# Attention heads paired across two key groups, and the spread of the inverse row sums on VectorE

## What is computed

```python
def _L0_attn_ref(X, Wq, Wk, Wv, Wpost):      # 16 heads in 4 groups
    Q = (X @ Wq).reshape(n, s, 4, 4, 64)     # (group, head of the group, width)
    K = (X @ Wk).reshape(n, s, 4, 64)        # one key and one value per group
    V = (X @ Wv).reshape(n, s, 4, 64)
    raw = einsum('bsgwe,btge->bstgw', Q, K / 8)
    attn = softmax(raw, axis=2)
    A = einsum('bstgw,btge->bsgwe', attn, V).reshape(n, s, 1024)
    return X + A @ Wpost

x = x + attention(xn) * silu(mixture_of_64_experts(xn))       # layer 0
x = x + state_space_model(xn) * silu(forest_of_8_trees(xn))   # layer 1
```

## Time and profile before

| | |
|---|---|
| median of three runs | 2696.54 us (2693.64 to 2705.16) |
| profiled execution, its own time | 2710.37 us |
| span of the profile | 2708.3 us |
| PE, matmuls (busy) | 2271.3 us, 84% of the span |
| DVE (VectorE) | 1850.7 us, 68% |
| ACT (ScalarE) | 1767.2 us, 65% |
| POOL (GpSimd) | 1738.4 us, 64% |
| PE clock granted, mean | 0.94 |

### The profile page before, as it was taken

How to read it: one execution, slowest core, us unless ns; L and a number is a source line. 1 busy time by engine, 2 the same in 40 slices (tenths; PEclk the granted TensorE clock), 3 DMA queues, 4 the chain that set the end, 5 groups by cost and what they waited for, 6 DMA issues and landing times.

```text
span 2708.3 us, 38199 instructions
## 1 busy us (share of the span) xinstructions
PE 2271.3 (84%) x13192; PEld 1417.2 (52%) x13192; DVE 1850.7 (68%) x2832; ACT 1767.2 (65%) x3278; POOL 1738.4 (64%) x1416
## 2 busy tenths in 40 slices
PE   5777879999688889799989898989888988987781
PEld 4444557775444456455644465546544644554351
DVE  5778544543246786687578766876777667788888
ACT  3556534446277876788677867785887677766762
POOL 1000254425757997788788879876987797655565
PEclk9888989999899999999989998999999999998895
DMA  4000258874555676555665475447543844476776
GB/s 158 24 20 6 88 156 237 235 219 77 102 110 120 129 154 155 110 115 122 162 122 103 111 167 115 100 104 172 111 100 84 191 105 86 94 172 151 172 183 143
DMA packets 282032, 344.50 MB, mean 127 GB/s; under 512 B 66159, under 2 KB 211504, under 8 KB 281840
## 3 DMA queue, kind: packets, MB, share of 16 engines
q0 software_dynamic: 84080, 175.67, 34.7%
q1 hardware_dynamic: 175248, 144.83, 18.2%
q10 hardware_dynamic: 22512, 21.57, 2.4%
HBM read 198.26 MB, written 26.80 MB: 83 GB/s over the span
## 4 chain that ended last, share of the span: by engine, by line
PE 26%; POOL 15%; issue 11%; DVE 10%; ACT 9%; DMA 1%; POOLq 0%; DVEq 0%; SPq 0%; ACTq 0%
POOL arena L1661 6%; PE bank L1913 4%; PE bank L1944 4%; POOL acc_sb L1639 4%; DVE bank L1536 4%; POOL arena L1667 3%; POOL arena L1677 2%; PE bank L1739 2%; PE bank L1786 2%; PE bank L1779 2%; PE bank L1836 2%; PE bank L1798 2%; ACT Pr L1043 2%; DVE arena L1502 1%; ACT bank L1160 1%
## 5 line engine op out<-in xcount | busy, mean ns | idle before, releaser
L1661 POOL TENSOR_TENSOR arena<-arena 128x512 f32<-128x512 f32 x512 | 874.3, 1785 | 18.2 <-DVE arena L1527 9.5
L1639 POOL DMA_INDIRECT acc_sb<-ybuf,slot_idx x256 | 422.5, 1650 | 132.6 <-DMA ybuf<-arena 60.8
L1252 DVE TENSOR_REDUCE negmax<-bank 128x1 f32<-128x512 f32 x512 | 339.8, 680 | 240.8 <-PE bank L1779 239.2
L1160 ACT ACTIVATE bank<-arena,A_sb 128x512 f32<-128x512 f32 x512 | 353.4, 694 | 149.8 <-DVE arena L1541 131.2
L1043 ACT ACTIVATE Pr<-bank,negmax 128x512 f32<-128x512 f32 x512 | 358.5, 700 | 135.1 <-DVE negmax L1252 133.6
L1667 POOL TENSOR_TENSOR arena<-arena 128x512 f32<-128x512 f32 x192 | 297.5, 1550 | 231.5 <-DVE arena L1536 231.2
L1536 DVE TENSOR_TENSOR_SCAN bank<-bank,arena 128x512 f32<-128x512 f32 x320 | 390.0, 1219 | 67.1 <-ACT bank L1160 61.2
L1786 PE MATMUL bank<-ident,Pr 128*128 128x128 f32 x2048 | 341.1, 291 | 79.2 <-ACT PT L1025 77.5
L1786 PEld LDWEIGHTS bank<-ident,Pr 128*128 128x128 f32 x2048 | 229.1, 145 | 317.6 <-ACT PT L1025 181.1
L1025 ACT COPY PT<-bank 128x512 f32<-128x512 f32 x512 | 303.3, 592 | 128.6 <-PE bank L1786 101.0
L1779 PE MATMUL bank<-Kp,Qp 64*128 64x512 f32 x1024 | 301.5, 666 | 70.9 <-ACT Pr L1043 59.2
(11 more groups left out here) (216 smaller groups left out, 3773.7 us busy)
## 6 DMA issues: line engine op xcount, KB each, us to landing
arena<-arena POOLq DMA_DIRECT2D x255, 512.0 KB, 5.3
arena<-bc_dram SPq DMA_DIRECT2D x256, 256.0 KB, 3.8
ybuf<-arena ACTq DMA_DIRECT2D x64, 256.0 KB
arena<-in_w_gate SPq DMA_DIRECT2D x64, 128.0 KB
arena<-in_w_up SPq DMA_DIRECT2D x64, 128.0 KB
arena<-in_w_down SPq DMA_DIRECT2D x64, 128.0 KB
arena<-in_X SPq DMA_DIRECT2D x8, 512.0 KB, 8.4
s_sb<-in_X SPq DMA_DIRECT2D x8, 512.0 KB
```

The lines of the kernel that those rows point to most:

```text
L1160: act.activation(bank[DECAY[g % 2]][:, :], dt_sb[:, size_slot(b, cb), :], ACT.Exp, scale=A_sb[:, cb, n:n + 1]).then_inc(ssm_decay, 1)
L1252: dve.tensor_reduce(negmax[:, m % RING_STAT:m % RING_STAT + 1], bank[m % RING_S_ATT][:, :], AX.X, ALU.max, negate=True).then_inc(att_max, 1)
L1639: pool.indirect_dma_start(acc_sb[:, i, :], None, ybuf, bass.IndirectOffsetOnAxis(ap=slot_idx[:, b * TILES + i, k:k + 1], axis=0), bounds_c ...
L1661: pool.tensor_tensor(st_sb[:, g % RING_S, :], u_sb[:, size_slot(b, cb), :], B_sb[:, load % RING_BC, :], ALU.mult).then_inc(ssm_input, 1)
```

## The change

It has two parts. The first pairs heads across two groups: pair p now holds head p mod 4 of group 2 t and head p mod 4 of group 2 t + 1, with t = p // 4 (`twin`). `Wq` and `Wpost` come permuted to suit. The two halves of `Kp` then hold two different groups, `Wk_sb` holds each column once, and one `Kp` serves four pairs. There are 2 key products and 2 key copies per batch in place of 4: the one in `att_lead`, and the one in pair 3. The second part moves the spread of the reciprocals from ScalarE to VectorE, right behind the reciprocal.

```diff
+TWINS = GROUPS // 2
...
-    Wk_sb = sb("Wk_sb", [P, KC, GROUPS * 2 * HD])
+    Wk_sb = sb("Wk_sb", [P, KC, GROUPS * HD])
...
+    def twin(p):
+
+        return p // HPG
...
-                for c in range(KC):
-                    for half in range(2):
-                        dst = Wk_sb[:, c, :].rearrange("p (g t d) -> p g t d", t=2, d=HD)[:, :, half, :]
-                        act.dma_start(dst, Wk[c * P:(c + 1) * P, :].rearrange("p (g d) -> p g d", d=HD)).then_inc(w_att, 16)
-                for dst, src in ((Wq_sb, Wq), (Wv_sb, Wv), (Wpost_sb, Wpost)):
+                for dst, src in ((Wk_sb, Wk), (Wq_sb, Wq), (Wv_sb, Wv), (Wpost_sb, Wpost)):
...
-                if at == K_AT and p + 1 < PAIRS and p % 2:
-                    self.copy_k(b, (p + 1) // 2, spare(n))
+                if at == K_AT and p + 1 < PAIRS and twin(p + 1) > twin(p):
+                    self.copy_k(b, twin(p + 1), spare(n))
...
-                p, at = n // PAIR_STEPS, n % PAIR_STEPS
-                if at == 1 and p >= 1:
-                    w.wait_ge(att_rec, PAIRS * b + p)
-                    w.wait_ge(att_invmm, PAIRS * b + p - 1)
-                    act.copy(rowinv[:, :, :], wide(rowrec[:, :], [[1, PAIR_STEPS], [0, HD]])).then_inc(att_inv, 1)
...
                     dve.reciprocal(rowrec[:, :], rowsum[:, p % 2, :]).then_inc(att_rec, 1)
+                    w.wait_ge(att_rec, use + 1)
+                    w.wait_ge(att_invmm, use)
+                    dve.tensor_copy(rowinv[:, :, :], wide(rowrec[:, :], [[1, PAIR_STEPS], [0, HD]])).then_inc(att_inv, 1)
...
-                    w.wait_ge(att_k, GROUPS * b + p // 2 + 1)
+                    w.wait_ge(att_k, TWINS * b + twin(p) + 1)
                     own = slice(j * HD, (j + 1) * HD)
-                    pe.matmul(bank[m % RING_S_ATT][:, :], Qp[own, p % 2, i * P:(i + 1) * P], Kp[own, p // 2 % 2, :], start=True, stop=True).then_inc(att_scored, 1)
+                    pe.matmul(bank[m % RING_S_ATT][:, :], Qp[own, p % 2, i * P:(i + 1) * P], Kp[own, twin(p) % 2, :], start=True, stop=True).then_inc(att_scored, 1)
...
-                g = p // 2
                 for c in range(TILES):
                     for j in range(2):
+                        g = 2 * twin(p) + j
                         ins = pe.matmul(bank[AV][j * HD:(j + 1) * HD, i * P:(i + 1) * P], V_sb[:, c, g * HD:(g + 1) * HD], PT[:, (m + j) % RING_P, c, :],
                                         start=(c == 0), stop=(c == TILES - 1))
...
-                if at == K_AT and p + 1 < PAIRS and p % 2:
-                    self.product_k(b, (p + 1) // 2, n)
+                if at == K_AT and p + 1 < PAIRS and twin(p + 1) > twin(p):
+                    self.product_k(b, twin(p + 1), n)
```

More of the change, by code:

```diff
@@ L643, in build_program @@
     pool_const, dve_tri, dve_path, a_exp, a_ok = (sem(n) for n in ("pool_const", "dve_tri", "dve_path", "a_exp", "a_ok"))
-    W_FIRST, W_SMALL, W_ATT, W_SSM = 16 * 5, 16 * 7, 16 * 7, 16 * 4
+    W_FIRST, W_SMALL, W_ATT, W_SSM = 16 * 5, 16 * 7, 16 * 4, 16 * 4
     dve_stats, pool_rsqrt = sem("dve_stats"), sem("pool_rsqrt")
@@ L1001, in att_v, with copy_k @@
                     act.copy(V_sb[:, i - 1:i + 1, :].rearrange("p a b -> p (a b)"), bank[2 + i // 2][:, :]).then_inc(att_v, 1)
-            def copy_k(self, b, g, bk):
-                w.wait_ge(att_kmm, GROUPS * b + g + 1)
-                w.wait_ge(att_scored, ATT_STEPS // GROUPS * (GROUPS * b + g - 1))
-                act.activation(Kp[:, g % 2, :], bank[bk][:, :], ACT.Copy, scale=HD ** -0.5).then_inc(att_k, 1)
+            def copy_k(self, b, t, bk):
+                w.wait_ge(att_kmm, TWINS * b + t + 1)
+                w.wait_ge(att_scored, ATT_STEPS // TWINS * (TWINS * b + t - 1))
+                act.activation(Kp[:, t % 2, :], bank[bk][:, :], ACT.Copy, scale=HD ** -0.5).then_inc(att_k, 1)
             def copy_q(self, b, p, bk):
@@ L1740, in product, with product_k @@
                 return ins
-            def product_k(self, b, g, n):
+            def product_k(self, b, t, n):
                 w.wait_ge(att_exp, b * ATT_STEPS + n - 1)
-                self.product(Wk_sb[:, :, g * P:(g + 1) * P], spare(n)).then_inc(att_kmm, 1)
+                self.product(Wk_sb[:, :, t * P:(t + 1) * P], spare(n)).then_inc(att_kmm, 1)
             def product_q(self, b, p, n):
@@ L1762, in score @@
                 pair, at = n // PAIR_STEPS, n % PAIR_STEPS
-                if at > K_AT and pair % 2 and pair + 1 < PAIRS:
-                    w.wait_ge(att_k, GROUPS * b + (pair + 1) // 2 + 1)
+                if at > K_AT and pair + 1 < PAIRS and twin(pair + 1) > twin(pair):
+                    w.wait_ge(att_k, TWINS * b + twin(pair + 1) + 1)
                 if at > SPREAD_AT:
@@ L2022, in host_layout @@
     chunk = lambda v: v.reshape(-1, P).T
+    paired = np.arange(HEADS * HD).reshape(TWINS, 2, HPG, HD).transpose(0, 2, 1, 3).reshape(-1)
     path = np.zeros((P, 2 * P), f)
@@ L2049, in host_layout @@
     return {
-        "X": d["L0_attn_X"], "Wq": d["L0_attn_Wq"], "Wk": d["L0_attn_Wk"], "Wv": d["L0_attn_Wv"], "Wpost": d["L0_attn_Wpost"],
+        "X": d["L0_attn_X"], "Wq": d["L0_attn_Wq"][:, paired], "Wk": d["L0_attn_Wk"], "Wv": d["L0_attn_Wv"], "Wpost": d["L0_attn_Wpost"][paired],
         "gateT": d["L0_ffn_gate_w"].T, "gate_bias": d["L0_ffn_gate_bias"], "w_gate": d["L0_ffn_w_gate"], "w_up": d["L0_ffn_w_up"],
```

## The result

Ten runs of each kernel gave a median of 2708.88 us (2704.52 to 2713.82) for the change and 2695.98 us (2689.60 to 2705.16) for the kernel before. The ratio is **1.0043, 95% interval [1.0028, 1.0058]**: the change made the kernel slower by 13 us (difference of the medians). That is inside the range given (2655 to 2720 us) and inside the half per cent called "same", but the sign is the other one: 11 us faster was forecast.

The account below looks back on a forecast made before the run. Four engines in lockstep, PE the fullest, were taken to wait for each other in turn. Key products -25.6, spread off ScalarE -5.6, spread on VectorE +15.4 and POOL held +4.6 gave -11 us: 2686 us, range 2655 to 2720 us.

Parts of the forecast that it names:

- The key products: Attention steps on PE and ACT: 16 of 32 products and their copies go, 1.6 us each, -26 us.
- So the loss is on the path wherever ACT or PE is: Attention step: ACT loses 1.7 us per key product, waiting and copying, before the next exponential; 1.6 us taken for each.
- the sum: Whole kernel: -25.6 - 5.6 + 15.4 + 4.6 = -11 us, giving 2686 us.
- The low bound, -11 us: Key products: 35 us of PE work counted only at PE's share of the chain, 0.31, gains 11 us.
- the products are hidden anyway: Rival: the scan's circle of POOL, ACT and DVE sets the pace, attention only fills; +3 us, 2700 us, chance 0.17.
- the slower rival: VectorE between reciprocal and scan: the copy waits out POOL's unbroken run; +21 us, 2718 us, chance 0.2.
- the prediction's own sign: Stretch beside the scan, 900 to 2400 us: if it grows, the prediction is wrong on the exchange of the copies.
- The spread leaves ScalarE: ScalarE: 64 copies, 39.7 us of work, go; at ACT's share of the chain, 0.14, -6 us.
- The high bound of 14 us: Spread leaving ScalarE: 39.7 us at 0.35, if ACT's share beside attention is that of PE.
- The spread arrives on VectorE: VectorE: 70 us of copies and waits at 0.22, +15 us (4 to 48); POOL held meanwhile, +5 us (0 to 20).
- VectorE has slack at the row maximum: VectorE's row maximum waited 239 us in all for TensorE's scores, so the arriving copy costs no more than +15 us.
- Its condition, a mean wait of 1.7 us: Slower rival decides once 48 copies take 2.1 us each, 1.7 us of it waiting, putting 40 us on the path.

Follow-up runs that it names:

- e1: The changed kernel with the spread back on ScalarE, so the pairing of heads alone: 2701.64 us against 2709.22 for the kernel before, 0.9975.
- e2: The kernel before with only the spread moved to VectorE, all 32 key products kept: 2725.70 us, 1.0069 to the kernel before.
- f4: The kernel before with the 24 key products inside attention steps done twice on TensorE: 2744.48 us, 1.0107 to the kernel before.
- f1: The changed kernel run once more, in another set as reference on the same chip: 2718.73 us, 1.0020 to the kernel before.
- f3: The changed kernel with a VectorE memset of the 128 x 512 tile in place of the spread copy: 2693.02 us, 0.9927 to the kernel before.
- f2: The changed kernel with the spread left out, its tile a constant 1: 2679.75 us against 2711.33 for the kernel before, 0.9875.
- g1: The kernel before with the spread left out and its 32 key products kept: 2687.60 us against 2696.53 for the kernel before, 0.9966.
- e3: The changed kernel with no spread copy; TensorE reads reciprocal columns with stride 0, eight products replacing four transpositions: 2697.22 us, 0.9954 to the kernel before.

## Why the prediction was wrong

**The key products (-26 us).** This is the term that failed. The quantities held: 16 products and copies gone, ScalarE's idle time 35.0 to 13.6 us. The step that failed is "So the loss is on the path wherever ACT or PE is", which priced each product at 1.6 us, and with it the sum, which took this term and the spread as independent. `e1` measured 0.4 us a product (-7 us) with the spread on ScalarE, and `e2` beside the change 0.4 to 0.8 (-7 to -13 us) with it on VectorE. 1.5 us came out only in the kernel without a spread. The price of 1.6 us was not far off for the product itself: where TensorE kept its higher clock level, 1.2 us came out with the spread on ScalarE.

Two things were missing. The sum had no term for the clock, which is 0.934 in `e1` where it is 0.942 before; by the relation within the kernel before that is some 12 of the 19 us that `e1` fell short, an estimate that no run tests. And with the copy on VectorE in the same steps the product is worth 0.6 us, half as much.

The low bound, -11 us by PE's share of the chain, was nearer than the value taken. The rival "the products are hidden anyway", 2700 us, is as near to the time (2709 us) as the slower rival's 2718, but not by its reason: `f4` shows that a product more costs 1.2 us. By the prediction's own sign it was wrong on the exchange as well, since the time beside the scan grew by 4 us (7 in `f1`). But `e2` shows 9 us of growth there for the exchange, about what its +14 us for the whole kernel stand for; it was the products that gave back only 2 to 6 us there, where 12 x 1.6 = 19 were forecast.

**The spread leaves ScalarE (-6 us).** The work gone was forecast right (39.7 us). It is worth 9 us beside 32 products, a weight of 0.23, and 27 us beside 16, a weight of 0.68; the term was 0.14. Beside the scan alone it is 10.8 and 16.2 us for some 30 us of copies, 0.36 and 0.54. The high bound of 14 us held in the one case and not in the other.

**The spread arrives on VectorE (+15 us, and +5 for POOL held).** 70 us of busy time were forecast, 72 to 76 were measured, with the shortest and the mean length as said. The weight of 0.22 was too low: 28 us of 76 (0.37) unpaired and 39 of 76 (0.52) paired, where 20 were forecast for both terms and 48 was the high bound of the first. The argument that "VectorE has slack at the row maximum" took the sum of a wait over all steps for slack at this one. POOL's own wait for the scan did stay near 231 us (235.7), as forecast.

**The exchange as a whole.** The sum had -6 + 15 + 5 = +14 us; `e2` gives +19 without the pairing, and the change against `e1` +12 to +18 (1.0020 and 1.0043 less 0.9975). The net came out right by luck: the credit was too small by a factor of 1.6 to 5 and the charge by 1.4 to 2. The sign of the forecast turned on the products alone: with -7 to -10 in place of -26 the sum is +4 to +7 us, and the two sets measured +5 and +12.

**The slower rival.** Its mechanism, the copy's wait for POOL, is there (the copy of 3.23 us above, and `f1` against `f3`), though not for POOL's whole unbroken run. Its condition, a mean wait of 1.7 us, is not: the mean is 1.13 - 0.43 = 0.70 us. The copies did cost about 40 us (39, `f1` against `f2`), by a higher weight and not by a longer wait. This is where the Trainium skill's page SBUF — State Buffer, "SBUF: two separate sides", was to decide: it has VectorE's copy and GpSimd block each other for a whole instruction. The trace agrees for the copy, whose 19 long cases all end 0.29 to 0.36 us behind one of POOL's products, though some waited for more than one (two at 2352.14 us, four in `f1`). The memset (485 ns in 64 of 64 cases) shows that not every write is held.

**Not settled.** The load of the keys' weight was costed at nothing and not tried by itself; the profiles show no gain from it, since the first exponential begins at 48.1 us before and at 51.2 and 49.7 us in the change and `f1`. Why the spread on ScalarE costs 27 us beside 16 products and 9 us beside 32 is shown in part only: 5 of the 18 us stand beside the scan and about 9 behind the last exponential, and in both the clock differs. Why the paired kernels with a spread run at the lower clock, and how much time that costs, was not tried. A copy on VectorE in a form that does not wait for POOL was not tried.

## What to carry to other kernels

Where several engines wait for each other in turn, don't price an edit by its engine's share of the chain over its busy share: those weights were 0.14 to 0.31 here, and work inside the attention step measured 0.23 to 0.68. When two pieces of work are taken out singly and give less than together, one may mask the other, as VectorE's copy did here. But first compare the granted clock of the timed runs, and the length of a stretch that the change doesn't touch: most of what looked like masking by ScalarE's spread went with the clock. And before moving a small copy to VectorE beside a busy GpSimd, look whether GpSimd can do it: the wait cost more here than the copy's own length.

## What the hardware showed unexpectedly

- VectorE's memset of 128 x 512 took 485 ns in 64 of 64 cases beside POOL, while a copy of 128 x 16 elements took from 175 to 3159 ns at the same place. The small copy was held up and the large memset was not, so here it goes by the kind of instruction and not by the size.
- The long copy shown above begins while POOL has only a DMA instruction under way (2351.60 to 2352.54), in front of its product's record (2352.14 against 2352.21), and still ends behind the second of its two products. POOL's records are rough, so who was first by 0.07 us is not settled.
- TensorE at the lower of its clock levels for 3.4 us made one pair of heads 1.3 us longer by the pairing (`e1`), where the same pair got 1.0 us shorter at the higher level (`f2`).
- The stretch behind the last exponential, with the same work on VectorE, ScalarE and POOL, took 316.5 us at a granted clock of 0.84 and 322.9 us at 0.81 (`f2`, `g1`).
- A second value from the same kernel: the longest copy was 6.08 us in `f1`, behind four products of POOL in a row, with the median where it was:

```profile
L1259 DVE COPY rowinv<-rowrec x64: 426/539/6082, 80.2 to 2391.0; 128x512 f32<-128x512 f32 x64
```

- TensorE takes a column with stride 0 as its stationary operand (`e3`), so the spread needs no tile. But 8 matmuls of 64 columns for 4 of 128 leave `e3` at 0.9954 where `f2` has 0.9875: 0.79%, 21 us, across two sets.
